# One-hot rows of a gate on GpSimd, and the sum of an attention taken by ScalarE

## The reference

```python
zs = -jnp.sort(-x, axis=-1)
cssv = jnp.cumsum(zs, axis=-1) - 1.0
support = zs > cssv / rho
k = jnp.maximum(jnp.sum(support, axis=-1, keepdims=True), 1)
tau = jnp.take_along_axis(cssv, k - 1, axis=-1) / k
attn = jnp.clip(x - tau, 0.0)                  # 16 heads, 256 x 77 each
...
_, idx = jax.lax.top_k(logits + lb_bias, K)    # K = 2 of E = 8
w = jax.nn.sigmoid(sel_logits)
w = w / (jnp.sum(w, axis=-1, keepdims=True) + 1e-06)
onehot = jax.nn.one_hot(idxf, E)
we = jnp.einsum('nke,nk->ne', onehot, wf)
hidden = jnp.square(jax.nn.relu(...))          # 256 -> 256 per expert
```

## Time and profile before

| what | us |
|---|---|
| median of 3 runs (lowest, highest) | 976.02 (974.1, 976.25) |
| the profiled execution, its own time | 975.64 |
| its span, first to last instruction | 973.8 |
| TensorE busy | 824.5 (85%) |
| VectorE busy | 732.9 (75%) |
| ScalarE busy | 592.3 (61%) |
| GpSimd busy | 528.8 (54%) |
| one steady turn, 476.90 to 530.20 | 53.30 |
| mean granted TensorE clock in that turn, share of full | 1.00 |

### The profile page before, as it was taken

The page is one execution under the profiler, slowest core; times in us unless marked ns, Lnnn a source line. Parts: engine busy times, 40 slices in busy tenths (PEclk is TensorE's granted clock), DMA queues, the critical chain, the costliest instruction groups (busy, mean ns, idle before and its releaser), DMA issues.

```text
span 973.8 us, 14666 instructions
## 1 busy us (share of the span) xinstructions
PE 824.5 (85%) x4960; PEld 687.1 (71%) x4960; DVE 732.9 (75%) x1892; ACT 592.3 (61%) x882; POOL 528.8 (54%) x476
## 2 busy tenths in 40 slices
PE   2250749999998989999999989898999999889998
PEld 1130527877787878878787878787787878668887
DVE  1478686888979888888888898888888878944222
ACT  1366574767677686767666766767676767553321
POOL 3447572757465665747575646657474757433010
PEclk9765667999999999999999999999999999989999
DMA  7100001010201001010102020010101010101010
GB/s 239 53 1 14 0 11 48 12 58 1 69 2 44 26 12 59 12 58 13 58 2 69 1 66 5 12 59 11 59 12 58 1 55 2 55 1 46 10 56 11
DMA packets 16182, 33.59 MB, mean 34 GB/s; under 512 B 1979, under 2 KB 12904, under 8 KB 14056
## 3 DMA queue, kind: packets, MB, share of 16 engines
q1 hardware_dynamic: 13760, 27.61, 9.0%
q0 software_dynamic: 1248, 4.73, 1.5%
q10 hardware_dynamic: 1096, 0.29, 0.2%
HBM read 28.30 MB, written 4.33 MB: 33 GB/s over the span
## 4 chain that ended last, share of the span: by engine, by line
PE 38%; DVE 32%; issue 11%; ACT 8%; POOL 8%; DMA 2%; ACTq 0%; DVEq 0%; POOLq 0%
PE y_ps L725 12%; PE h_ps L712 9%; PE s_ps L669 6%; DVE fsum L852 6%; PE m_ps L677 4%; DVE g L995 4%; POOL over L309 4%; ACT signs L462 4%; DVE asum L883 4%; DVE first L966 3%; DVE fold_a L849 3%; PE m_ps L685 3%; PE m_ps L628 3%; DVE fold_b L856 2%; ACT hid L508 2%
## 5 line engine op out<-in xcount | busy, mean ns | idle before, releaser
L309 POOL TENSOR_TENSOR over<-S,tau 128x1232 f32<-128x1232 f32 x128 | 286.1, 2251 | 209.9 <-DVE tau L868 207.4
L725 PE MATMUL y_ps<-w_sb,hid 128*128 128x256 f32 x1152 | 280.6, 387 | 50.6 <-ACT hid L508 46.2
L725 PEld LDWEIGHTS y_ps<-w_sb,hid 128*128 128x128 f32 x1152 | 213.7, 191 | 98.2 <-ACT hid L508 67.3
L712 PE MATMUL h_ps<-x1nT,w_sb 128*128 128x256 f32 x1152 | 277.6, 384 | 0.0
L712 PEld LDWEIGHTS h_ps<-x1nT,w_sb 128*128 128x128 f32 x1152 | 216.2, 192 | 30.5 <-issue 3.0
L464 ACT ACTIVATE over<-over 128x1232 f32<-128x1232 f32 x128 | 155.7, 1228 | 4.5 <-POOL over L309 1.5
L852 DVE TENSOR_REDUCE fsum<-over 128x16 f32<-128x1232 f32 x96 | 137.3, 1430 | 23.5 <-ACT over L464 23.5
L508 ACT ACTIVATE hid<-g 128x512 f32<-128x512 f32 x144 | 89.9, 625 | 92.6 <-DVE g L995 92.1
L995 DVE SCALAR_TENSOR_TENSOR g<-h_ps,sw_all 128x512 f32<-128x512 f32 x128 | 87.3, 683 | 55.3 <-PE h_ps L712 40.6
L462 ACT ACTIVATE signs<-over 128x1232 bf16<-128x1232 f32 x96 | 117.1, 1220 | 18.9 <-POOL over L309 18.9
L476 ACT ACTIVATE attnT<-s_ps 77x512 f32<-77x512 f32 x128 | 65.9, 591 | 71.8 <-PE s_ps L669 71.8
(11 more groups left out here) (100 smaller groups left out, 1037.3 us busy)
## 6 DMA issues: line engine op xcount, KB each, us to landing
sw_all<-sw_scratch SPq DMA_DIRECT2D x16, 1024.0 KB, 5.2
x_sb<-in_x SPq DMA_DIRECT2D x16, 256.0 KB, 2.7
w_sb<-in_w POOLq DMA_DIRECT2D x2, 2048.0 KB, 12.0
out_y<-y SPq DMA_DIRECT2D x16, 256.0 KB, 5.5
ctx_sb<-in_ctx SPq DMA_DIRECT2D x16, 77.0 KB
wk_sb<-in_wk SPq DMA_DIRECT2D x1, 256.0 KB
wv_sb<-in_wv SPq DMA_DIRECT2D x1, 256.0 KB
wq_sb<-in_wq SPq DMA_DIRECT2D x1, 256.0 KB
```

The costliest lines, as they stand in the source:

```text
L309: return pool.tensor_tensor(dst, S[:, p, t], tau[:, p, t].rearrange("p (h o) -> p h o", o=1).broadcast_to([P, NH, NK]), ALU.subtract)
L712: last = pe.matmul(h_ps[:, i % 2, c, :], w1_sb[:, e, k, c * P:(c + 1) * P], x1nT[:, p, k, :], start=(k == 0), stop=(k == KC - 1))
L725: last = pe.matmul(y_ps[:, t, :], hid[:, i % 2, c, t * P:(t + 1) * P], w2_sb[:, e, c, :], start=(i == 0 and t == 0 and c == 0), stop=(i == ...
```

## The change

Four things.

The one-hot part of the gate leaves VectorE. GpSimd now casts the two best places to float, subtracts them from `iota` for both places at once (`apart`), compares with zero, adds the two rows (`chosen`) and masks the sigmoids (`wsel`). In its queue these five stand between the two subtractions of round 1. VectorE only sums and takes the reciprocal (`late_weights`, behind `new_values`); 1e-6 is a ninth column of `wsel`, so its addition falls away. `wnorm` moves to GpSimd, ahead of the power.

The row sums of the final attention are taken by ScalarE as the accumulated output of its relu, one sum over all 16 heads of a token in the place of 16 sums. VectorE's `asum` falls away.

The tolerance is summed over the heads too (`tol_sum`, one small instruction of VectorE), with a quarter of the factor. GpSimd makes the verdict (two instructions of 2 elements) behind the second subtraction and ahead of `wnorm` and the power.

The count on TensorE takes two matmuls of one column instead of one.

```diff
-            for t, v in ((ones, 1.0), (half_pow, 0.5), (neg_half_pow, -0.5)):
+            for t, v in ((ones, 1.0), (half_pow, 0.5), (neg_half_pow, -0.5), (wsel[:, :, E:], 1e-6)):
...
+            def mid_verdict(m):
+                pool.wait_ge(attn_ready.sem, attn_ready.at(m))
+                pool.wait_ge(check_chain.sem, check_chain.at(m, 4))
+                pool.wait_ge(count_done.sem, count_done.at(m - 1))
+                pool.tensor_tensor(unsettled[:], asum[:], tol_sum[:], ALU.subtract).then_inc(check_chain.sem, 1)
+                pool.wait_ge(check_chain.sem, check_chain.at(m, 5))
+                pool.tensor_scalar(unsettled[:], unsettled[:], -float(NH), 0.0, ALU.add, ALU.is_gt
+                                   ).then_inc(unsettled_known.sem, 1)
+            def late_pick(m):
+                pool.wait_ge(gate_chain.sem, gate_chain.at(m))
+                pool.tensor_copy(best_f[:], best_at[:, :, 0:2]).then_inc(pick_chain.sem, 1)
...
+                pool.tensor_tensor(apart[:],
+                                   iota[:].rearrange("p (a b e) -> p a b e", a=1, b=1).broadcast_to([P, T, 2, E]),
+                                   best_f[:].rearrange("p t (j o) -> p t j o", o=1).broadcast_to([P, T, 2, E]),
+                                   ALU.subtract).then_inc(pick_chain.sem, 1)
...
+                pool.tensor_scalar(apart_all, apart_all, 0.0, None, ALU.is_equal).then_inc(pick_chain.sem, 1)
...
+                pool.tensor_tensor(chosen[:], apart[:, :, 0], apart[:, :, 1], ALU.add).then_inc(pick_chain.sem, 1)
...
+                pool.tensor_tensor(wsel[:, :, 0:E], sigm[:], chosen[:], ALU.mult).then_inc(pick_chain.sem, 1)
             def late_weight_roots(m):
+                pool.wait_ge(w_chain.sem, w_chain.at(m))
+                pool.tensor_tensor(wnorm[:], wsel[:, :, 0:E],
+                                   wrec[:].rearrange("p (t o) -> p t o", o=1).broadcast_to([P, T, E]),
+                                   ALU.mult).then_inc(w_ready.sem, 1)
...
                     new_residual(b, p)
-                    for t in range(T):
-                        subtract(b, p, 1, t)
+                    subtract(b, p, 1, 0)
+                if late:
+                    late_pick(b - 2)
+                if new:
+                    subtract(b, p, 1, 1)
+                if mid:
+                    mid_verdict(b - 1)
                 if late:
                     late_weight_roots(b - 2)
...
-                act.activation(attn[:, t], attn[:, t], ACT.Relu).then_inc(attn_ready.sem, 1)
+                act.wait_ge(unsettled_known.sem, unsettled_known.at(m - 1))
+                act.activation(attn[:, t], attn[:, t], ACT.Relu, accum_out=asum[:, t:t + 1]
+                               ).then_inc(attn_ready.sem, 1)
...
-                pe.matmul(y_ps[0:1, 0, 0:1], unsettled_any[:], ones[:], start=True, stop=True
-                          ).then_inc(count_done.sem, 1)
+                for t in range(T):
+                    last = pe.matmul(y_ps[0:1, 0, 0:1], unsettled[:, t:t + 1], ones[:], start=(t == 0),
+                                     stop=(t == T - 1))
+                last.then_inc(count_done.sem, 1)
...
-            def mid_check(m):
-                for t in range(T):
-                    dve.tensor_reduce(asum[:, t * NH:(t + 1) * NH], attn[:, t], AX.X, ALU.add
...
+            def mid_tolerance_sum(m):
+                dve.wait_ge(check_chain.sem, check_chain.at(m, 3))
+                dve.wait_ge(unsettled_known.sem, unsettled_known.at(m - 1))
+                dve.tensor_reduce(tol_sum[:], tol[:], AX.X, ALU.add).then_inc(check_chain.sem, 1)
...
+            def late_weights(m):
+                dve.wait_ge(pick_chain.sem, pick_chain.at(m))
+                dve.tensor_reduce(wsum[:], wsel[:], AX.X, ALU.add).then_inc(w_chain.sem, 1)
+                dve.wait_ge(w_chain.sem, w_chain.at(m, 1))
+                dve.wait_ge(w_ready.sem, w_ready.at(m - 1))
+                dve.reciprocal(wrec[:], wsum[:]).then_inc(w_chain.sem, 1)
...
                 gates(7)
+                if mid:
+                    mid_tolerance_sum(b - 1)
                 if late:
                     late_gate(b - 2)
                 if new:
                     new_values(b, p)
+                if late:
+                    late_weights(b - 2)
                 gates(8)
-                if mid:
-                    mid_check(b - 1)
```

More of the change, by code:

```diff
@@ L86, in xattn_moe_kernel @@
         iota = sb("iota", [P, E])
-        zeros = sb("zeros", [P, T, 2])
         ones = sb("ones", [P, 1])
@@ L114, in xattn_moe_kernel @@
         spare_f, spare_n, spare_r = (sb(f"spare_{n}", [P, T * NH]) for n in "fnr")
-        tol, asum, unsettled = (sb(n, [P, T * NH]) for n in ("tol", "asum", "unsettled"))
-        unsettled_any = sb("unsettled_any", [P, 1])
+        tol = sb("tol", [P, T, NH])
+        asum, tol_sum, unsettled = (sb(n, [P, T]) for n in ("asum", "tol_sum", "unsettled"))
         unsettled_count = sb("unsettled_count", [1, 1], I32)
@@ L129, in xattn_moe_kernel @@
         best_at, best_f = sb("best_at", [P, T, 8], U32), sb("best_f", [P, T, 2])
-        first, chosen = sb("first", [P, T, E]), sb("chosen", [P, T, E])
-        sigm, wsel = sb("sigm", [P, T, E]), sb("wsel", [P, T, E])
+        apart = sb("apart", [P, T, 2, E])
+        chosen = sb("chosen", [P, T, E])
+        sigm, wsel = sb("sigm", [P, T, E]), sb("wsel", [P, T, E + 1])
         wsum, wrec, wnorm = sb("wsum", [P, T]), sb("wrec", [P, T]), sb("wnorm", [P, T, E])
@@ L791, in _ @@
         def _(dve):
-            for t, v in ((v_pad, 0.0), (signs[:, :, :, :, NK:SW - 1], 26.0), (signs[:, :, :, :, SW - 1:], 25.0),
-                         (zeros, 0.0)):
+            for t, v in ((v_pad, 0.0), (signs[:, :, :, :, NK:SW - 1], 26.0), (signs[:, :, :, :, SW - 1:], 25.0)):
                 dve.memset(t[:], v).then_inc(consts, 1)
@@ L876, in mid_magnitude @@
                 dve.wait_ge(tau_ready.sem, tau_ready.at(m))
-                dve.scalar_tensor_tensor(tol[:], tau_m, -1.0, tau_m, ALU.mult, ALU.max).then_inc(check_chain.sem, 1)
-            def mid_check(m):
-                for t in range(T):
-                    dve.wait_ge(attn_ready.sem, attn_ready.at(m, t + 1))
-                    dve.tensor_reduce(asum[:, t * NH:(t + 1) * NH], attn[:, t], AX.X, ALU.add
-                                      ).then_inc(attn_summed.sem, 1)
-                dve.wait_ge(check_chain.sem, check_chain.at(m, 3))
[L886 to L890, removed]
+                dve.wait_ge(check_chain.sem, check_chain.at(m - 1))
+                dve.scalar_tensor_tensor(flat(tol[:]), tau_m, -1.0, tau_m, ALU.mult, ALU.max
+                                         ).then_inc(check_chain.sem, 1)
+            def mid_tolerance_sum(m):
+                dve.wait_ge(check_chain.sem, check_chain.at(m, 3))
+                dve.wait_ge(unsettled_known.sem, unsettled_known.at(m - 1))
+                dve.tensor_reduce(tol_sum[:], tol[:], AX.X, ALU.add).then_inc(check_chain.sem, 1)
             def late_verdict(m):
@@ L960, in late_gate @@
                 last.then_inc(gate_chain.sem, 1)
[L961 to L975, removed]
-                dve.tensor_reduce(wsum[:], wsel[:], AX.X, ALU.add).then_inc(gate_chain.sem, 1)
-                dve.wait_ge(gate_chain.sem, gate_chain.at(m, 8))
-                dve.tensor_scalar(wsum[:], wsum[:], 1e-6, None, ALU.add).then_inc(gate_chain.sem, 1)
-                dve.wait_ge(gate_chain.sem, gate_chain.at(m, 9))
-                dve.reciprocal(wrec[:], wsum[:]).then_inc(gate_chain.sem, 1)
-                dve.wait_ge(gate_chain.sem, gate_chain.at(m, 10))
-                dve.wait_ge(sw_ready.sem, sw_ready.at(m - 1))
-                dve.tensor_tensor(wnorm[:], wsel[:],
-                                  wrec[:].rearrange("p (t o) -> p t o", o=1).broadcast_to([P, T, E]),
-                                  ALU.mult).then_inc(w_ready.sem, 1)
+            def late_weights(m):
[4 more added lines that the diff above has]
+                dve.reciprocal(wrec[:], wsum[:]).then_inc(w_chain.sem, 1)
             def old_gates(f, p, i):
```

19 lines of the change are left out of this document (14 added, 5 removed).

## The result

| | before | now |
|---|---|---|
| median of 5 runs | 975.1 | 987.43 (981.57 to 3056.62) |
| the profiled execution, its span | 975.64, 973.8 | 993.89, 991.9 |
| ratio of the times, 95% interval | | 1.0133 (1.0101 to 1.0164) |
| VectorE busy, GpSimd busy | 732.9, 528.8 | 623.5, 553.8 |

The change makes the kernel 1.3% slower, and six further executions later gave 991.91 (988.83 to 998.2), a ratio of 1.0193 (1.0163 to 1.0224). The forecast, 975.4 in 971.5 to 983, missed. One execution of the five took 3056.62; the ratio leaves it out, and it is taken up among the experiments.

A forecast was written before the change was run, and what follows sets the result against it. Two nearly equal loops into `y_ps` bound the kernel, through VectorE's count and GpSimd's power. Steady turns -0.96, turns 2 and 3 +0.97, about 0.3 back later: -0.29 from 975.64 gives 975.35, likeliest 975.4, range 971.5 to 983.

The forecast's parts named there:

- Eight small instructions: On GpSimd between the start of the subtractions and the power: 1.83 us a turn, 2.33 with gaps between chained steps.
- TensorE's wait for the count: At TensorE's first layer-2 group, waiting for VectorE's reading of unsettled rows: 0.35 us a turn, expected to go.
- new wait for `sw`: On TensorE at the turn-over, waiting for GpSimd's power: some 2 us expected in every turn.
- A turn at full clock: Steady turn: turn-over +0.18, count +0.12, slack at `y_ps` -0.38, so -0.08 us.
- the count's second column: On TensorE, a second matmul for the count, expected to delay keys and `hid` by 0.12 us.
- ScalarE's accumulated sum: On ScalarE's relu: between nothing and 0.2 us each, taken as an extra instruction of 0.2, hidden.
- `fold_a` was not held by the power: On VectorE behind `y`: `fold_a` was expected held to the end of GpSimd's power, 523.75, the count read near 527.8.
- rival (d): TensorE's clock falls from idling about 2.0 at the turn-over; losing 1.8 us a turn gives 1000; chance 0.01.
- Rival (a): GpSimd's eight small instructions cost more and lengthen the loop through its power; 985.6 at 0.32 each; chance 0.26.
- Rival (c): VectorE's loop was the only one; count read 1.6 us earlier in 13 turns, giving 955; chance 0.02.
- Rival (b): GpSimd's small instructions lie at their floor; up to 0.38 us a turn gained, 971 to 973.5; chance 0.25.
- (e): Summed tolerance counts settled rows as unsettled; 18 spare steps cost over 240 us per such batch; chance 0.01.

The follow-up runs named there:

- The gate alone: Only the pick and wnorm moved to GpSimd, attention sums and verdict left on VectorE, against the kernel before the change: median 964.76, ratio 0.9903.
- sum-alone kernel: Only ScalarE's sum, the summed tolerance and GpSimd's verdict, one-hot work left on VectorE, against the kernel before the change: median 976.93, ratio 1.003.

## Why the prediction was wrong

The mechanics of a turn held. Eight small instructions: 1.83 forecast, 1.82 measured. Power after the subtraction's start: 6.79 forecast (the text's 6.8), 6.76 measured. TensorE's wait for the count: gone. Its new wait for `sw`: "some 2 us", measured 2.02. A turn at full clock: -0.08 forecast, -0.17 measured; most of the difference is the count's second column, 0.12 forecast and 0.05 measured. ScalarE's accumulated sum as an extra instruction of 0.2: 0.20 measured. One detail was wrong without effect: `fold_a` was not held by the power (0.48 beside it, 532.03 in the rows above), so `y`'s end set the order and not the power's.

The step that failed is the weight of rival (d), "TensorE idles about 2.0 at the turn-over, against 1.83 now, which kept 2.4 GHz", held at 0.01. The 2.0 was my own number, and I took it as good as 1.83. It is not: idle 1.41 and 1.49 and the 1.83 of before kept 1.00 in all twelve turns; 2.00 to 2.04 lost the clock in nine to eleven of twelve turns, in three profiles of two kernels; 0.29 kept it. What decides between 1.83 and 2.02 was not separated further. Besides 0.19 of length, the places differ: the 1.83 stood ahead of the last `y_ps` group and had eight dense matmuls between it and the next turn's first waits, and the 2.02 stands ahead of the transposes. The earlier trace rows already showed that idle time can cost TensorE half its clock, at 4.73, and no row that I had read lay between 1.83 and 4.73. An unknown with that much room, in all of 13 turns, deserved a quarter of the chance and a range up to 1000.

The trace of before even held a warning that I had not read. In turn 2, with the clock at 1.00 from 118.8, TensorE waited 1.74 and the clock then stood at half from 125.4 to 128.8, so that eight matmuls took 3.65:

```profile
123.40 0.66 PE L669 MATMUL s_ps<-ident,attn 128*77 128x128 f32 x4 [1.74 <-ACT attnT L476]
123.99 1.49 PE L677 MATMUL m_ps<-attnT,v_pad 77*32 77x128 f32 x32
125.41 3.65 PE L685 MATMUL m_ps<-wo_sb,OT 128*128 128x256 f32 x8
```

The gate alone waited 1.79 at the same place and kept the clock there (these eight took 1.99). So a wait's length does not decide by itself: 1.74 lost the clock once where 1.83 never did in the steady turns. What the experiments show is narrower: in this one place, with this work around it, 1.49 keeps the clock and 2.03 loses it in 11 turns of 12.

The size in (d) was near: 1.8 a turn forecast; 1.54 to 1.68 in nine turns, 3.05 in one and nothing in two measured, 17.3 in all. The Trainium skill (TensorE: Matmul & The Clock Gate, HAM oscillation — how this bites in real kernels) describes this pattern: a wait between two groups of matmuls that throttles TensorE again in every iteration, so that the cost comes back each time. The traces agree that it comes back (clock 0.50 for 3.4 us behind most turn-overs, 6.8 behind one), and here at waits of 2.0, shorter than the 3 to 5 us that the Trainium skill gives there for its own kernel.

Rival (a), dearer GpSimd instructions, would have ended at the same side and did not happen (1.82; `wsel` took 0.22 and not 0.33). Its "about 986" for 0.33 apiece should have read about 987: 8 times 0.33 is 2.64, 0.81 too much, 11.3 in 14 turns on top of 975.35. Rival (c), a loop of VectorE alone, is refuted by its unchanged turn in the sum-alone kernel. Rival (b), cheaper GpSimd instructions, did not happen either. Of (e), the price held (255 a batch, over 240 forecast); whether it ever struck stays open.

I also summed the two parts as one. Apart, the gate gives -1.0% and the sum +0.3%; together they give +1.3 to +1.9%, since the verdict's 0.55 us lengthens the one gap on which the clock hangs.

## What to carry to other kernels

Where a change turns another engine's work into idle time of TensorE, write down the length of TensorE's idle stretch before and after, and look in the trace for the shortest stretch behind which the clock fell (here 1.74) and the longest that kept it (1.83). From the shorter of the two on, treat the clock as unknown and price it, because the loss comes back in every iteration. On the engine that TensorE waits for, put instructions that nobody needs yet (here a verdict of 0.55 us) behind the one that is waited for. A few matmuls of no use in a gap were worth 0.4 to 1.9% here, where they took less than the gap; eight that took more than it gave nothing. Measure one of them first.

## What the runs showed of the hardware

- The clock can fall after the wait that goes with the loss: in the turns shown above it was 1.00 through the idle 2.01 and fell when TensorE was at work again, to stay at 0.50 for 3.4 us or, once, 6.8. In the idle 4.73 of turn 16, before the change, it fell earlier, while TensorE still did nothing (work began again at 860.61):

```profile
858.50:860.50 2.00, 0.00 (x0) 0.00 (x0) 2.00 (x4) 0.57 (x1) 0.00 (x0) 0.69 0.00 0
```

- One matmul of 128x256 in f32 as the kernel writes it stands in the trace as two instructions: four written ones are the x8 of L829 above. It costs 0.43 us (eight in 3.45), twice what I had taken from rows of eight in 1.9.
- ScalarE's accumulated sum is an instruction of its own behind the activation:

```profile
522.46 0.20 ACT L508 ACTIVATION_READ_ACCUMULATOR attn<-attn 128x1 f32 x1
```

- GpSimd's small instructions differ little, cast and four-dimensional broadcast included: 0.19 to 0.24 for 2 or 4 elements, 0.22 for 16, 0.24 and 0.31 for 32. The power is the exception: 2.93 for 16.

```profile
L363 POOL CAST best_f<-best_at x16: 184/186/187, 141.3 to 947.1; 128x4 f32<-128x4 uint32 x16
L365 POOL TENSOR_TENSOR apart<-iota,best_f x16: 239/240/243, 141.6 to 947.3; 128x32 f32<-128x32 f32 x16
L371 POOL TENSOR_SCALAR apart<-apart x16: 308/308/310, 141.9 to 947.7; 128x32 f32<-128x32 f32 x16
```
